# Keeping the third head group's masked scores in PSUM in a fused cross-attention and mixture-of-experts kernel

## The chip, the cores and the metric

One core of a Trainium2 chip runs the whole program. Its engines work side by side, each through its own list of instructions, and wait for each other by semaphores: TensorE (PE; matmuls and transposes, results in PSUM), ScalarE (ACT), VectorE (DVE), GpSimd (POOL), and the queue of SyncE (SP), which issues DMAs. SBUF and PSUM are the on-chip memories; PSUM has eight banks of 128 x 512 fp32. The metric is the device time of one execution in microseconds, lower is better.

## The reference

Eight sequences of 112 tokens (hidden size 512) attend to a context of 375 rows of width 128. The causal mask leaves only context rows 0 to 111 in use. Then follows a feed-forward block of eight experts (two per token) and one shared expert. The part that the change touches:

```python
qp = q @ Wq.T
k, v = jnp.split(latent_kv @ Wkv_expand.T, 2, axis=-1)
# 16 heads of 32
scores = jnp.einsum('bhqd,bhkd->bhqk', qh, kh) * inv_sqrt_d
scores = jnp.where(causal, scores, jnp.finfo(scores.dtype).min)
attn = jax.nn.softmax(scores, axis=-1)
out = jnp.einsum('bhqk,bhkd->bhqd', attn, vh)
x = x + out @ Wout.T            # then: x = x + ffn(layernorm(x))
```

## The kernel before

All engines are programmed by hand; the order of the instructions on each is the order of the code. A batch `b` (0 to 7) is one sequence. Its 16 heads are numbered `h = 4c + r`: four *head groups* `r` (0 to 3), each with four heads `c`. Group `r` has the PSUM bank `S[r]`, in which its four heads' scores (112 x 112 each) lie side by side. The other four banks are A, B, CC and D.

One batch goes through these steps:

- `scores(b)` on TensorE (L635): 16 matmuls write all four banks S[0] to S[3]; the last round over `r` tells group by group that it is done.
- `masked(b, r)` on VectorE (L1341): four operations add the mask, negate, and leave each row's extreme in `negmax`. For `r < RP` the result goes back into the bank; for the others into an SBUF tile `score{r}`. `RP` is 2 (L138).
- `exps(b, r)` on ScalarE (L1053): four exponentials, each followed by a read of its accumulator, with the row's sum; input from the bank for `r < RP`, else from `score{r}`.
- `inverse(b, r)` on VectorE (L1347), then `normalised(b, r)`, on GpSimd (L439) except for the first two of batch 0.
- `transposed(b, r)` on TensorE (L624) into bank A or B, `put_pT(b, r)` (L1008 on ScalarE; group 1 from batch 2 on is at L1351 on VectorE) copies it to `probT`.
- `v_proj(b + 1)` and P·V (L773) on TensorE; `put_oT(b)` (L1064) on ScalarE and `oT_lo(b)` (L1379) on VectorE split its result, `out_proj` (L563) uses it.

TensorE's loop over `b` is: `scores(b+1)`, `transposed(b, 0)` and `(b, 1)`, then in batches 0 and 1 projections of queries and keys for the second half, later `out_proj(b-2)`; `transposed(b, 2)` and `(b, 3)`; `v_proj(b+1)`; P·V. ScalarE's is: `put_pT(b, 0)` (and 1 in batches 0 and 1), `exps(b+1, 0)`, in batches 0 and 1 `put_pT(b, 2)` and `(b, 3)`, `exps(b+1, 1)`, later `put_x2T`, `put_pT(b, 2)` and `(b, 3)` here; `exps(b+1, 2)`, `put_oT(b)`, `exps(b+1, 3)`. VectorE's is: `inverse(b+1, 0)`, `put_pT(b, 1)` from batch 2 on, `masked(b+1, 3)`, `inverse(b+1, 1)`, layer-norm and residual work, `put_v(b+1)`, `inverse(b+1, 2)`, `oT_lo(b)`, `masked(b+2, 0)`, `inverse(b+1, 3)`, `masked(b+2, 1)`, `masked(b+2, 2)`.

The waits around the four banks use the same `RP` (L632 and L1337):

```python
pe.wait_ge(s["mask"], R * (b + 1))         # ahead of scores(b + 1): all four groups of b masked
pe.wait_ge(s["exp"], R * (b - 1) + RP)     # in scores(b): exponentials of b - 1, groups below RP
if b > 0 and r >= RP:                      # in masked(b, r): the SBUF tile must have been read
    dve.wait_ge(s["exp"], R * (b - 1) + r + 1)
```

Behind the attention the feed-forward stages run on the same engines; the loads of the experts' weights start when the output projections are done.

Of the kernel before, what the change touches and what calls it, by code (L numbers as in the profile page):

```python
# [43 lines left out]
def build(nc, x, ctxT, wqT, wkvT, woT, gateT, guT, dnT, sguT, sdnT, out):  # L44
# [5 lines left out]
    R = P // HD  # L50
# [84 lines left out]
    kT = [m.inside(att, f"kT{i}", [P, C, W]) for i in range(NBLK)]  # L135
    v_sb = m.inside(att, "v_sb", [SQ, H])
    score_at = [sg_end + 4 * 2 * H, shared_end - 4 * 2 * H]
    RP = 2  # L138
    score = [None] * RP + [m.inside(score_at, f"score{r}", [SQ, C, SQ]) for r in range(RP, R)]
    prob = [m.inside(att, f"prob{r}", [SQ, C, SQ]) for r in range(R)]  # L140
    probT = [m.inside(att, f"probT{r}", [SQ, C, SQ]) for r in range(R)]
# [123 lines left out]
    s = {n: nc.alloc_semaphore(f"s_{n}") for n in names}  # L265
# [3 lines left out]
    with nc.Block() as block:  # L269
# [280 lines left out]
        def _(pe):  # L550
# [55 lines left out]
            def wait_probT(b, r):  # L606
                if b < 2:
                    pe.wait_ge(s["probT"], R * b + r + 1)
                elif r == 1:
                    pe.wait_ge(s["probT_v"], b - 1)  # L610
                else:
                    pe.wait_ge(s["probT"], R * 2 + (R - 1) * (b - 2) + (1 if r == 0 else r))

            def transposed(b, r):
                if b == 0 and r < RP:
                    pe.wait_ge(s["prob"], r + 1)
                else:
                    pe.wait_ge(s["prob_p"], R * b + r + 1 - RP)
                if r == 0:
                    pe.wait_ge(s["Vs"], b + 1)  # L620
                if r >= 2:
                    wait_probT(b, r - 2)
                for c in range(C):
                    ins = pe.transpose((A, B)[r % 2][0:SQ, c * SQ:(c + 1) * SQ], prob[r][:, c, :], ident[0:SQ, 0:SQ])  # L624
                ins.then_inc(s["PT"], 1)

            def scores(b):
# [3 lines left out]
                if b > 0:  # L631
                    pe.wait_ge(s["exp"], R * (b - 1) + RP)  # L632
                for r, c in [(r, c) for c in range(C) for r in range(R)]:
# [82 lines left out]
            for b in range(NB):  # L716
# [9 lines left out]
                if b == 0:  # L726
                    pe.wait_ge(s["KT"], C + 1)
                    k_proj(1, 1, CC)

                transposed(b, 0)  # L730
                if b == 0:
                    pe.wait_ge(s["QT"], C + 2)
                transposed(b, 1)
                if b == 0:
                    q_proj(1, 2, D)
# [9 lines left out]
                if b >= 2:  # L745
# [6 lines left out]
                    early = 9 if b + 1 < NB else 6  # L752
                    out_proj(b - 2, 0, early)
                transposed(b, 2)
                if b >= 3:
                    t2(b - 3, CC)
# [10 lines left out]
                for h in range(NH):  # L767
                    r, c = h % R, h // R
# [237 lines left out]
        def _(act):  # L1006
# [40 lines left out]
            def exps(b, r):  # L1047
# [3 lines left out]
                for c in range(C):  # L1051
                    src = S[r][0:SQ, c * SQ:(c + 1) * SQ] if r < RP else score[r][:, c, :]
                    ins = act.activation(prob[r][:, c, :], src, ACT.Exp, bias=negmax[:, r, c:c + 1], scale=-1.0,  # L1053
# [228 lines left out]
        def _(dve):  # L1282
# [51 lines left out]
            def masked(b, r):  # L1334

                dve.wait_ge(s["S"], R * b + r + 1)
                if b > 0 and r >= RP:  # L1337
                    dve.wait_ge(s["exp"], R * (b - 1) + r + 1)
# [366 lines left out]
```

## Time and profile before

| | us |
|---|---|
| three timed executions | 340.15, 342.38, 342.55 |
| their median | 342.38 |
| the profiled execution, as timed | 341.11 |
| its span, first to last instruction | 339.2 |
| mean granted TensorE clock | 0.995 of full |

Each number below comes from one profiled execution. A stretch is given in microseconds from the start of its span. "Busy" is the time in which an engine worked on at least one instruction; neighbouring instructions overlap by their pipeline, so the price of one more in a row is the distance from start to start, not its duration. Instructions of one line that follow each other may be merged into one row, with their count.

### The profile page before, as it was taken

The page shows a single profiled execution, that of the slowest core. Times are in us where ns is not written, and L with a number is a line of the kernel's source. Part 1 is how long each engine was busy: PE and PEld are TensorE (multiplying, and loading weights), DVE is VectorE, ACT ScalarE, POOL GpSimd, SP SyncE. Part 2 cuts the span into 40 slices and gives each one's busy share as a digit, 9 for nine tenths or more (in the row PEclk, how much of TensorE's full clock was granted, in tenths as well). Part 3 has the DMA queues.
Part 4 walks back from the last instruction along what each step waited for, and adds up shares of the span by engine and source line. Part 5 has one row for each costly group of instructions (what it writes and reads, how often), then busy time and mean ns, then how long its engine had stood idle before and what let it go on. Part 6 is the DMA issues. An engine that isn't in the chain of part 4 may idle for free.

```text
span 339.2 us, 7025 instructions
## 1 busy us (share of the span) xinstructions
PE 323.4 (95%) x2285; PEld 279.1 (82%) x2285; DVE 269.3 (79%) x676; ACT 232.3 (68%) x581; POOL 140.7 (41%) x144
## 2 busy tenths in 40 slices
PE   7999998999999999999999999999999999999981
PEld 6898886777786798989888977888889999899981
DVE  4879779999756268885667999999999999899840
ACT  3666999999844134131225788888898999889831
POOL 3335475888842000343500008767743423432421
PEclk9999999999999999999999999999999999999998
DMA  7999400000004799697599865554555465455243
GB/s 227 376 337 380 142 3 3 3 3 0 3 2 182 266 348 363 272 308 272 220 283 242 247 242 94 122 119 85 99 116 121 85 110 129 97 90 116 46 50 44
DMA packets 31794, 53.00 MB, mean 156 GB/s; under 512 B 7440, under 2 KB 14992, under 8 KB 30736
## 3 DMA queue, kind: packets, MB, share of 16 engines
q1 hardware_dynamic: 27616, 43.34, 39.1%
q0 software_dynamic: 4144, 9.23, 15.7%
q8 instruction: 19, 0.31, 0.4%
q14 instruction: 15, 0.12, 0.1%
HBM read 32.22 MB, written 16.92 MB: 145 GB/s over the span
## 4 chain that ended last, share of the span: by engine, by line
PE 68%; ACT 10%; DMA 8%; DVE 5%; issue 2%; SPq 2%; POOL 2%; POOLq 1%; ACTq 0%; DVEq 0%
PE bank L563 28%; PE bank L893 19%; ACT prob L1053 6%; PE bank L917 4%; DMA out<-y_sb,dest 3%; PE bank L921 3%; DMA w_dn<-dnT 2%; PE bank L624 2%; PE bank L931 2%; PE bank L927 2%; PE bank L787 2%; PE bank L555 2%; SPq L348 1%; PE bank L773 1%; DMA act_w<-act_e 1%
## 5 line engine op out<-in xcount | busy, mean ns | idle before, releaser
L542 POOL DMA_INDIRECT out<-y_sb,dest x21 | 46.5, 2215 | 101.6 <-ACT y_sb L1223 60.3
L1297 DVE TENSOR_TENSOR gu_parts<-w_gu,gu_parts 128x704 fp32r<-128x704 f32 x84 | 77.2, 953 | 0.3 <-ACT gu_parts L1008 0.3
L1008 ACT ACTIVATE gu_parts<-w_gu 128x704 fp32r x84 | 66.0, 792 | 10.9 <-PE bank L893 10.2
L893 PE MATMUL bank<-gu_parts,xsT_hi 128*128 128x352 f32 x328 | 71.0, 338 | 0.0
L893 PEld LDWEIGHTS bank<-gu_parts,xsT_hi 128*128 128x128 f32 x328 | 54.3, 188 | 5.5 <-issue 4.1
L893 PE MATMUL bank<-gu_parts,xsT_lo 128*128 128x352 f32 x164 | 39.6, 322 | 0.0
L563 PE MATMUL bank<-x2T_hi,w_sg_lo 128*128 128x512 f32 (+1 forms) x88 | 32.6, 371 | 0.1
L563 PE MATMUL bank<-x2T_hi,w_sg_hi 128*128 128x512 f32 (+1 forms) x88 | 32.0, 363 | 0.0
L563 PE MATMUL bank<-x2T_lo,w_sg_hi 128*128 128x512 f32 (+1 forms) x88 | 31.9, 363 | 0.0
L439 POOL TENSOR_TENSOR prob<-prob,rrow 112x448 f32<-112x448 f32 x30 | 27.4, 933 | 9.9 <-DVE rrow L1347 9.8
L515 POOL DMA_INDIRECT xs_dram<-x2n,slot_i x14 | 14.4, 1026 | 37.1 <-DVE eid L1595 33.2
L893 PEld LDWEIGHTS bank<-gu_parts,xsT_lo 128*128 128x128 f32 x164 | 28.6, 188 | 0.0
L1297 DVE TENSOR_TENSOR dn_lo<-w_dn,dn_hi 128x1024 fp32r<-128x1024 f32 x21 | 25.6, 1218 | 3.3 <-ACT dn_hi L1008 3.3
L1008 ACT ACTIVATE act_s_hi<-act_s 128x512 fp32r<-128x512 f32 (+1 forms) x10 | 5.8, 577 | 31.7 <-DVE act_s L1494 24.7
L1514 DVE TENSOR_TENSOR xres<-xres,bank 128x512 f32<-128x512 f32 x35 | 23.0, 683 | 5.0 <-PE bank L563 4.6
L1008 ACT ACTIVATE dn_hi<-w_dn 128x1024 fp32r x21 | 22.2, 1059 | 5.5 <-PE bank L921 4.2
L1053 ACT ACTIVATE prob<-score,negmax 112x112 f32<-112x112 f32 x64 | 24.5, 419 | 0.0
L1053 ACT ACTIVATE prob<-bank,negmax 112x112 f32<-112x112 f32 x64 | 21.9, 384 | 2.5 <-DVE negmax L1341 2.5
L563 PEld LDWEIGHTS bank<-x2T_hi,w_sg_lo 128*128 128x128 f32 x88 | 16.5, 188 | 4.1 <-issue 1.7
L563 PEld LDWEIGHTS bank<-x2T_hi,w_sg_hi 128*128 128x128 f32 x88 | 16.5, 188 | 1.8
L563 PEld LDWEIGHTS bank<-x2T_lo,w_sg_hi 128*128 128x128 f32 x88 | 16.5, 188 | 1.7
L917 PE MATMUL bank<-dn_lo,actT_split_hi 128*128 128x512 f32 x40 | 16.0, 399 | 1.4 <-DVE dn_lo L1297 0.9
(216 smaller groups left out, 818.8 us busy)
## 6 DMA issues: line engine op xcount, KB each, us to landing
w_gu<-guT SPq DMA_DIRECT2D x8, 1408.0 KB, 9.4
xs_dram<-no_row SPq DMA_DIRECT2D x1, 5460.0 KB, 19.8
xs_in<-xs_dram SPq DMA_DIRECT2D x21, 256.0 KB, 2.9
w_dn<-dnT SPq DMA_DIRECT2D x8, 512.0 KB, 6.4
act_w<-act_e SPq DMA_DIRECT2D x19, 176.0 KB, 2.2
w_sg<-sguT SPq DMA_DIRECT2D x10, 256.0 KB, 5.1
w_dn<-dnT SPq DMA_DIRECT2D x8, 192.0 KB, 7.0
w_sd<-sdnT SPq DMA_DIRECT2D x5, 256.0 KB, 4.8
```

What stands on the lines that cost most here:

```text
L439: pool.tensor_tensor(prob[r][:, :, :], prob[r][:, :, :], rrow[:, r, :].unsqueeze(2).to_broadcast([SQ, C, SQ]), ALU.mult)\
L515: pool.indirect_dma_start(out=xs_dram[:, :], out_offset=bass.IndirectOffsetOnAxis(ap=slot_i[:, k, n:n + 1], axis=0), in_=x2n[:, n, :], in_ ...
L542: pool.indirect_dma_start(out=out[:, :], out_offset=bass.IndirectOffsetOnAxis(ap=dest[:, i, 0:1], axis=0), in_=y_sb[i % 2][:, :], in_offse ...
L555: ins = pe.transpose(dst[:, c * P:(c + 1) * P], src[:, c * P:(c + 1) * P], ident[:, :])
L563: ins = pe.matmul(dst, a, b, start=start and n == 0, stop=stop and n == len(passes) - 1)
L893: ins = pe.matmul(dst[:, 0:F], xsT[x_][:, c, :], gu2[w_][:, c, f0:f0 + F], start=c == 0 and n == 0, stop=c == C - 1 and n == 2)
L917: pe.matmul(A[:, :], actT_split[0][:, k, :], dn2[part][:, k, :], start=k == 0 and part == 1, stop=False)
L921: ins = pe.matmul(A[:, :], actT_split[1][:, k, :], dn2[0][:, k, :], start=False, stop=False)
L1008: act.activation(dst, src, ACT.Copy).then_inc(s[sem], 1)
L1053: ins = act.activation(prob[r][:, c, :], src, ACT.Exp, bias=negmax[:, r, c:c + 1], scale=-1.0, accum_out=rowsum[:, r, c:c + 1])
L1297: dve.tensor_tensor(lo_, src, hi_.bitcast(F32), ALU.subtract).then_inc(s[sem], 1)
L1514: dve.tensor_tensor(xres[:, n, :], xres[:, n, :], (B, CC, D, A)[i][:, :], ALU.add)\
```

## The change

`RP` goes from 2 to 3. Group 2's masked scores are written back to bank S[2] in place of an SBUF tile `score2`, the exponentials of group 2 read that bank, `scores(b)` waits for the exponentials of groups 0 to 2 of the batch before, and `masked(b, 2)` has no wait for exponentials any more. In `transposed`, where `RP` stood for the number of groups that VectorE normalises in batch 0, a constant `RN = 2` keeps the value. The order of the instructions is the same on every engine. The SBUF region of `score2` is left free; `score3` and what follows it there lie lower. All lines behind L138 have a number that is one higher.

```diff
-    RP = 2
+    RP = 3
+    RN = 2
     score = [None] * RP + [m.inside(score_at, f"score{r}", [SQ, C, SQ]) for r in range(RP, R)]
...
             def transposed(b, r):
-                if b == 0 and r < RP:
+                if b == 0 and r < RN:
                     pe.wait_ge(s["prob"], r + 1)
                 else:
-                    pe.wait_ge(s["prob_p"], R * b + r + 1 - RP)
+                    pe.wait_ge(s["prob_p"], R * b + r + 1 - RN)
```

## Rows read from the trace of the kernel before

**Rows 1.** Busy time by stretch: us, busy of each engine (instructions), clock, DMA share, GB/s.

```profile
66.00:74.00 8.00, 8.00 (x105) 6.00 (x103) 7.54 (x43) 7.93 (x38) 6.41 (x7) 1.00 0.00 0
90.00:180.00 90.00, 89.88 (x502) 75.43 (x495) 56.42 (x118) 30.89 (x58) 23.32 (x36) 1.00 0.69 244
...
331.00:334.00 3.00, 0.97 (x10) 0.83 (x8) 0.00 (x0) 0.95 (x2) 1.27 (x1) 1.00 0.09 16
334.00:339.00 5.00, 0.00 (x0) 0.00 (x0) 0.00 (x0) 0.00 (x0) 0.28 (x1) 0.69 0.43 52
```

**Rows 2.** Chain of waits, batch 2: start us, us, what.

```profile
47.47 1.75 ACT prob L1053 x9
...
50.45 0.44 ACT oT_hi L1064
...
54.26 0.60 DVE probT L1351
```

**Rows 3.** TensorE's timeline: L635 is `scores`, L624 `transposed`; idle time before in brackets.

```profile
33.11 1.05 PE L635 MATMUL bank<-kT,qT 32*112 32x112 f32 x32 [0.15 <-ACT prob L1053]
...
38.30 0.93 PE L624 MATMUL bank<-ident,prob 112*112 112x112 f32 x8
...
41.34 1.05 PE L635 MATMUL bank<-kT,qT 32*112 32x112 f32 x32
...
45.86 0.93 PE L624 MATMUL bank<-ident,prob 112*112 112x112 f32 x8
...
49.13 1.05 PE L635 MATMUL bank<-kT,qT 32*112 32x112 f32 x32
...
55.00 0.57 PE L624 MATMUL bank<-ident,prob 112*112 112x112 f32 x4 [0.63 <-DVE probT L1351]
...
57.80 1.05 PE L635 MATMUL bank<-kT,qT 32*112 32x112 f32 x32
```

**Rows 4.** Chain of waits, end of batch 5.

```profile
79.62 0.60 ACT probT L1008
80.26 0.96 PE bank L563 x3
```

**Rows 5.** ScalarE's timeline, batch 0: start us, us, engine, line, operation, out<-in.

```profile
32.48 0.40 ACT L1053 ACTIVATE prob<-bank,negmax 112x112 f32<-112x112 f32 x1
32.71 0.25 ACT L1053 ACTIVATION_READ_ACCUMULATOR prob<-bank,negmax 112x1 f32 x1
32.81 0.43 ACT L1053 ACTIVATE prob<-score,negmax 112x112 f32<-112x112 f32 x1
```

**Rows 6.** Steady batches, both timelines: ahead of `transposed(5, 2)`, and of `scores(7)`.

```profile
77.66 0.40 PE L563 MATMUL bank<-w_o_hi,oT_hi 128*128 128x512 f32 x1
78.03 0.60 PE L624 MATMUL bank<-ident,prob 112*112 112x112 f32 x4
...
81.21 0.44 ACT L1053 ACTIVATE prob<-score,negmax 112x112 f32<-112x112 f32 x1
...
81.58 0.43 ACT L1053 ACTIVATE prob<-score,negmax 112x112 f32<-112x112 f32 x1
81.86 0.25 ACT L1053 ACTIVATION_READ_ACCUMULATOR prob<-score,negmax 112x1 f32 x1
82.06 1.05 PE L635 MATMUL bank<-kT,qT 32*112 32x112 f32 x32
```

**Rows 7.** VectorE's timeline, masked scores of batch 3 (groups 0, 1, 2, 2).

```profile
51.46 0.27 DVE L1341 CUSTOM_DVE_ANT_0 bank<-bank,mask 112x112 f32<-112x112 f32 x1
...
53.12 0.32 DVE L1341 CUSTOM_DVE_ANT_0 bank<-bank,mask 112x112 f32<-112x112 f32 x1
...
53.35 0.27 DVE L1341 CUSTOM_DVE_ANT_0 score<-bank,mask 112x112 f32<-112x112 f32 x1
...
53.55 0.27 DVE L1341 CUSTOM_DVE_ANT_0 score<-bank,mask 112x112 f32<-112x112 f32 x1
```

**Rows 8.** ScalarE's timeline: `put_pT` of groups 2 and 3, batches 0 and 1.

```profile
38.88 0.98 ACT L1008 ACTIVATE probT<-bank 112x448 f32<-112x448 f32 x2
...
46.62 1.03 ACT L1008 ACTIVATE probT<-bank 112x448 f32<-112x448 f32 x2
```

## Prediction

> **What bounds the kernel now.** I read four views, in this order. First, the busy time by stretch, to see which stages have room. From 90 us on TensorE is busy for 89.88 of 90 us, with the clock granted in full [rows 1]: whatever moves the end of the attention stage moves the whole program behind it, one for one. From about 28 to 90 us the stage of the change runs, one batch in about 8 us, and there TensorE (8.00 of 8 us), ScalarE (7.93) and VectorE (7.54) are all nearly full [rows 1]. No single engine bounds it. What counts is the loop of waits between them.
>
> Second, the chain of waits says which loop. Up to 50.9 us it runs through ScalarE, whose exponentials and copies follow each other without a gap, then over `oT_lo` and the masked scores on VectorE to `probT` at 54.26 [rows 2], for which TensorE waits 0.63 us [rows 3]. From batch 3 on it alternates: ScalarE from `put_oT(b-1)` to `put_pT(b, 2)`, then TensorE's `v_proj` (80.26) and P·V [rows 4], which release the next `put_oT`. The exponentials of group 2 stand behind `put_pT(b, 3)`, in the shadow of `v_proj` and P·V, so they are not in that loop.
>
> Third and fourth, the timelines of ScalarE and VectorE for the price of one operation, and TensorE's for the place of each `scores`.
>
> **The change part by part.** No instruction moves on any engine. Three things change.
>
> (1) *ScalarE reads group 2 from PSUM.* From start to start, an exponential out of PSUM takes 0.33 us (32.48 to 32.81) [rows 5], one out of SBUF 0.37 us (81.21 to 81.58) [rows 6]. Four of them save 0.16 us a batch.
>
> (2) *VectorE writes group 2's masked scores to PSUM.* Start to start 0.23 us (53.12 to 53.35) against 0.20 us (53.35 to 53.55) [rows 7], so it pays 0.03 to 0.04 each, 0.15 us a batch. Its wait on the exponentials of the batch before goes, but that costs nothing now: nobody waited there.
>
> (3) *`scores(b+1)` waits for the exponentials of groups 0 to 2 of batch b, no longer 0 and 1.* S[2] holds the masked scores until ScalarE has read them, and `scores` overwrites all four banks. Everything behind it on TensorE (`transposed`, the projections, `v_proj`, P·V) waits with it, for TensorE takes its matmuls in order. The Trainium skill, "PSUM — Partial Sum Buffer", section "Summary: rules for kernel authors", says the same of the hardware: a bank that is being read must not be the target of a matmul at that time, and the guard goes by bank. So no looser wait is possible with this placement. By that page alone the wait is necessary, and only the rows tell whether it is also late.
>
> How late it is, batch by batch. The last exponential's accumulator read ends 0.48 us after the exponential starts (32.48 to 32.71 + 0.25 = 32.96), and TensorE starts 0.15 us later, at 33.11 [rows 3, 5].
>
> *scores(1).* Today it already waits for group 1 (that 0.15 us of idle time has ScalarE as its releaser) [rows 3]. Now it waits for group 2, which starts at 32.81: four at 0.33, the last at 33.80, ended at 34.28, `scores(1)` at 34.43. That is 1.32 us later. From there to `transposed(0, 2)` at 38.30 TensorE has no gap to give back, and ScalarE's copy of that result at 38.88 comes 0.58 us behind it [rows 3, 8]. So the copy moves to 40.20. ScalarE has nothing else it may do: the copies stand ahead of `exps(1, 1)` in its order. The head start from (1) is eaten by that wait.
>
> *scores(2).* From 40.20: two copies 0.85 (46.62 to 47.47 in a later batch) [rows 2, 8], group 1 4 x 0.33 = 1.32, group 2's last exponential 0.99 later, at 43.36, ended 43.84, `scores(2)` at 43.99 where it was at 41.34: 2.65 late. `transposed(1, 2)` moves from 45.86 to 48.51 [rows 3], ScalarE's copy to 49.09 (46.62 before) [rows 8]: 2.47 late, since 0.18 us of room was there.
>
> *scores(3).* From 49.09: 0.85 + 1.32 + 0.99 = 52.25, ended 52.73, `scores(3)` at 52.88 where it was at 49.13 [rows 3]: 3.75 late. Not all of it counts, because VectorE was the late one here. `masked(3, 0)` began at 51.46 [rows 7], and now waits for `scores(3)`: its matmuls run 1.05 us [rows 3] and the hand-over takes about 0.10, so it begins at 54.03, 2.57 late. From there VectorE needed 2.80 us to start `put_pT(2, 1)` at 54.26 [rows 2, 7]; with (2) it needs 2.95. That copy starts at 56.98, and `transposed(2, 3)` 0.74 us behind it, at 57.72 where it was at 55.00 [rows 3]: 2.72 late.
>
> *scores(4) and on.* `scores(4)` comes 2.80 us behind it, at 60.52 (57.80 before) [rows 3]. ScalarE, by the same terms, is through with group 2 of batch 3 by 57.72 + 0.58 + 0.42 + 0.99 + 0.48 + 0.15 = 60.34. So the new wait is hidden from here, by 0.18 us. In the steady batches it is nearer. At `scores(7)` the exponentials ended at 81.86 + 0.25 = 82.11; (1) makes that about 81.96 and with 0.15 the release 82.11, against a start at 82.06 [rows 6]. About 0.05 to 0.1 us late each time. Behind it stands a wait that absorbs this: `transposed(b, 2)` started at 78.03 where the matmul ahead of it started at 77.66 [rows 6], 0.37 us for what takes 0.23, thus 0.14 us of waiting on GpSimd. Should that cover be gone, four batches at 0.1 us make 0.4. (2) likewise lies in VectorE's own waits there; (1) saves time only in ScalarE's wait ahead of `put_oT`.
>
> Sum: +1.32 + (2.65 - 1.32 - 0.18) + (2.72 - 2.47) = about **+2.7 us**, all of it between 33 and 58 us. Beside the profiled execution's own 341.11 us this is 343.8. The timed runs lie at 340.15, 342.38 and 342.55; with the profiled one the middle is 341.75, so I say 344.4.
>
> **The rivals.**
>
> *The new wait is on the steady path too* (0.13). The rows leave only 0.05 to 0.18 us between cover and cost at four batches. If the hand-over takes 0.2 to 0.3 us more than at 33.11, each pays that: +0.8 to +1.2, 345.2 to 345.6, and with the late copies of (2) up to 346.8. For it: the margins above. Against: `transposed(b, 2)` waits for GpSimd, not for `scores`.
>
> *TensorE's clock falls* (0.03). TensorE would idle ahead of three `scores`: 0.15 + 1.32, 2.65 - 1.32 and 3.75 - 2.47, so about 1.5, 1.3 and 1.3 us. The trace keeps the full grant with 0.97 us of work in 3 us, and shows 0.69 only in the 5 us behind it without any matmul [rows 1]. A fall from 2.4 to 1.2 GHz over a 4 us stretch that is full would cost up to 4 us: 348. The Trainium skill, "TensorE: Matmul & The Clock Gate", section "What's actually happening", has idleness bring the throttle back; by that rule a stage with more gaps is exposed, but the trace's gap of 2 us at full grant speaks against it here.
>
> *The waits are mostly absorbed* (0.16). ScalarE may have more room at the copies of batches 0 and 1 than I see. Then only `scores(1)`'s 1.32 or less arrives, less the saving of (1) in three batches, 0.48: 341.75 + 1.32 - 0.48 = 342.6.
>
> *The saving of (1) decides, faster than before* (0.03). If ScalarE's order alone set the stage, as the chain suggests up to 50 us, 32 exponentials at 0.04 us give 1.3 us: 341.75 - 1.28 = 340.5. It decides if `scores` is never late by over its cover, 0.15 us; the first one is at 1.32 [rows 3, 5]. The Trainium skill's table of op costs ("VectorE: DVE Perf Modes", section on the TRN2 errata) gives ScalarE 224 cycles of fixed cost from SBUF and 172 from PSUM. The trace agrees in size. By that table alone the estimate is 32 x 52 cycles at 1.2 GHz, 1.4 us faster.
>
> **How the numbers follow.** The forecast (0.65) has its own range, 343.6 to 345.2: the three steps by 0.1 us each, and the half us that executions differ. The range 342.3 to 346.8 takes in most of the absorbed case and the steady one; it leaves out the clock and the faster case. One per cent, about what a measurement of this kernel can tell from no change, is 3.4 us. The forecast reaches it only at its upper edge or through the spread of the runs (0.06 of its 0.65); the steady and clock cases add 0.16. So slower 0.22, within 0.76, faster 0.02.
>
> **What would show it.** Right: idle time of over 1 us on TensorE ahead of the second, third and fourth `scores`, released by ScalarE's `prob`; ScalarE no longer full between 35 and 50 us, with waits for TensorE's transposes at the copies; `scores(4)` near 60.5 us; from there a period of 8.0 to 8.1 us as now. Exponentials from PSUM at 0.33 us in group 2, masked scores at 0.23. Wrong: `scores(4)` before 59 us (absorbed), a period over 8.2 us (steady path), or a granted clock below 1.00 between 33 and 60 us.

## The result, and the profile after

The changed kernel takes 343.35 us (median of 17 executions, 341.78 to 344.43), the kernel before 340.31 us (17 executions, 339.08 to 342.55). The ratio is 1.0082, 95% interval 1.0068 to 1.0096: 2.8 us slower (2.3 to 3.3; the medians lie 3.0 apart). The profiled execution spans 341.4 us at a mean granted clock of 0.996.

Three views of the changed kernel carry the reading. First the busy time by stretch (us, then PE, PEld, DVE, ACT, POOL, granted clock, DMA share, GB/s):

```profile
28.00:40.00 12.00, 10.43 (x114) 9.82 (x115) 11.00 (x70) 8.97 (x45) 6.77 (x9) 1.00 0.77 273
40.00:50.00 10.00, 8.39 (x108) 7.08 (x106) 6.43 (x41) 8.35 (x39) 5.91 (x6) 1.00 0.01 2
50.00:58.00 8.00, 6.36 (x89) 4.88 (x88) 6.36 (x42) 8.00 (x43) 4.30 (x6) 1.00 0.01 2
...
66.00:74.00 8.00, 7.98 (x102) 6.04 (x99) 7.59 (x44) 7.81 (x38) 6.41 (x8) 1.00 0.01 2
...
90.00:180.00 90.00, 89.89 (x523) 74.56 (x522) 57.34 (x128) 32.52 (x69) 24.79 (x39) 1.00 0.66 235
```

From 66 to 74 us TensorE's and VectorE's busy times are those of before to within 0.05 us, and ScalarE is a little less busy (7.81 us where [rows 1] has 7.93). From 90 to 180 us TensorE is as full as before; VectorE and ScalarE differ there by 0.9 and 1.6 us, since the attention stage now ends at 93.30 us, further into this stretch than the 90.09 of before. The holes are before 58 us: ScalarE works for 8.35 of the 10 us from 40 to 50. In the kernel before it had worked for all ten:

```profile
40.00:50.00 10.00, 9.49 (x164) 7.86 (x162) 7.09 (x43) 10.00 (x52) 6.89 (x7) 1.00 0.01 2
```

Second, TensorE's timeline, each `scores` (now L636) and the `transposed` of groups 2 and 3 (L625), with the idle time before it and who ended it:

```profile
28.04 1.05 PE L636 MATMUL bank<-kT,qT 32*112 32x112 f32 x32 [0.28 <-ACT qT L1025]
...
34.99 1.05 PE L636 MATMUL bank<-kT,qT 32*112 32x112 f32 x32 [1.53 <-ACT prob L1054]
...
44.60 1.05 PE L636 MATMUL bank<-kT,qT 32*112 32x112 f32 x32 [1.36 <-ACT prob L1054]
...
53.52 1.05 PE L636 MATMUL bank<-kT,qT 32*112 32x112 f32 x32 [1.36 <-ACT prob L1054]
...
58.18 0.57 PE L625 MATMUL bank<-ident,prob 112*112 112x112 f32 x4 [0.21 <-DVE probT L1352]
...
60.98 1.05 PE L636 MATMUL bank<-kT,qT 32*112 32x112 f32 x32
```

These answer to [rows 3]. The idle times of 1.53, 1.36 and 1.36 us, where before had 0.15 us and none, are all three ended by ScalarE's exponentials. In this execution everything started late, before the stage of the change: `scores(0)` stands at 28.04, in the one of before at 27.51. So I measure from `scores(0)`.

Third, ScalarE's timeline at the copies of transposed groups (L1009): groups 0 and 1 of batch 0, then groups 2 and 3 of batches 0 and 1, which answer to [rows 8]:

```profile
37.28 0.98 ACT L1009 ACTIVATE probT<-bank 112x448 f32<-112x448 f32 x2 [0.58 <-PE bank L625]
...
40.79 0.98 ACT L1009 ACTIVATE probT<-bank 112x448 f32<-112x448 f32 x2 [0.51 <-PE bank L625]
...
49.71 0.98 ACT L1009 ACTIVATE probT<-bank 112x448 f32<-112x448 f32 x2 [1.14 <-PE bank L625]
```

ScalarE stood idle here for 0.58, 0.51 and 1.14 us, waiting for transposes that stood on TensorE behind the late `scores`. That is the loop: `scores(b+1)` waits for ScalarE, then ScalarE waits for what stands behind `scores(b+1)`.

The stage, in microseconds from the start of `scores(0)`:

| | before | forecast | after |
|---|---|---|---|
| `scores(1)` | 5.60 | 6.92 | 6.95 |
| `scores(2)` | 13.83 | 16.48 | 16.56 |
| `scores(3)` | 21.62 | 25.37 | 25.48 |
| `transposed(2, 3)` | 27.49 | 30.21 | 30.14 |
| `scores(4)` | 30.29 | 33.01 | 32.94 |
| `scores(7)` | 54.55 | about 57.3 | 57.32 |
| first matmul of the feed-forward | 62.58 | 65.3 | 65.26 |

This stage length, 62.58 us before and 65.26 after (+2.68), is the measure that I use below beside the ratio. The timed ratios have intervals of 0.5 to 1.1 us to either side (1.3 us for the four-group kernel); the stage lengths come from one profiled execution each, so tenths between them may be chance, and they leave out what varies in the loads ahead and in the experts' DMAs behind.

### The profile page after: what moved, and what is told of

The parts are those of the page before. It is cut to its first block, busy times and chain, and to the rows that moved or that the text cites. A ratio compares the mean times of both kernels' runs of the same rounds, so it can differ in the third digit from the quotient of the medians.

```text
span 341.4 us, 7018 instructions
## 1 busy us (share of the span) xinstructions
PE 324.2 (95%) x2285; PEld 280.8 (82%) x2285; DVE 270.4 (79%) x676; ACT 232.0 (68%) x581; POOL 140.5 (41%) x144
## 4 chain that ended last, share of the span: by engine, by line
PE 80%; ACT 6%; DVE 4%; DMA 3%; issue 2%; POOL 2%; POOLq 1%; ACTq 0%; SPq 0%; DVEq 0%
PE bank L564 33%; PE bank L894 22%; PE bank L918 5%; PE bank L625 3%; ACT prob L1054 3%; PE bank L922 3%; PE bank L636 2%; PE bank L928 2%; PE bank L932 2%; PE bank L788 2%; PE bank L556 2%; DMA out<-y_sb,dest 1%; DMA w_kv<-wkvT 1%; PE bank L774 1%; PE bank L968 1%
## 5 line engine op out<-in xcount | busy, mean ns | idle before, releaser
L1009 ACT ACTIVATE gu_parts<-w_gu 128x704 fp32r x84 | 66.0, 792 | 11.1 <-PE bank L894 10.2
L1054 ACT ACTIVATE prob<-bank,negmax 112x112 f32<-112x112 f32 x96 | 32.8, 378 | 2.5 <-DVE negmax L1342 2.5
L1009 ACT ACTIVATE act_s_hi<-act_s 128x512 fp32r<-128x512 f32 (+1 forms) x10 | 5.8, 578 | 31.5 <-DVE act_s L1495 28.8
L1009 ACT ACTIVATE dn_hi<-w_dn 128x1024 fp32r x21 | 22.2, 1059 | 5.0 <-PE bank L922 3.9
L1342 DVE CUSTOM_DVE_ANT_0 bank<-bank,mask 112x112 f32<-112x112 f32 x96 | 22.9, 310 | 1.0 <-PE bank L636 0.8
L1054 ACT ACTIVATION_READ_ACCUMULATOR prob<-bank,negmax 112x1 f32 x96 | 22.2, 231 | 0.0
```

The lines of the kernel that those rows point to most:

```text
L1009: act.activation(dst, src, ACT.Copy).then_inc(s[sem], 1)
L1342: ins = dve.tensor_tensor_reduce(raw if r < RP else score[r][:, c, :], raw, mask[:, :], -1.0, LARGEST, ALU.add, ALU.min, negmax[:, r, c:c ...
```

## The experiments

Two theories stand against each other. The first: the loss is idle time at the wait of `scores(1)` to `scores(3)`, because these stand on TensorE at a time when ScalarE has group 2 still ahead of it. The second: the placement itself costs, through VectorE's dearer writes or something in PSUM that the trace of before does not show. A third question is whether batches 3 to 7 pay.

**The wait alone.** The kernel before, with this edit:

```diff
-                    pe.wait_ge(s["exp"], R * (b - 1) + RP)
+                    pe.wait_ge(s["exp"], R * (b - 1) + RP + 1)
```

> The kernel before with one edit: scores(b) waits for the exponentials of three groups, the masked scores of group 2 stay in SBUF. Theory (the wait is the loss): scores(1) to scores(3) are late as in the changed kernel and a little more, since group 2's exponentials keep their 0.37 us: 0.16 us later at each of the three waits; VectorE keeps its cheaper masked scores. The three waits then give about +2.7 + 3 x 0.16 - 0.15 = +3.0 us against before, and idle times of about 1.6 us ahead of scores(1) to (3). Rival (the loss comes from VectorE's dearer writes to PSUM, 0.15 us a batch on its path): under +1 us.

Measured: ratio 1.0111 (1.0079 to 1.0143), +3.8 us (2.7 to 4.9); stage +2.82 us. TensorE's timeline:

```profile
34.53 1.05 PE L635 MATMUL bank<-kT,qT 32*112 32x112 f32 x32 [1.64 <-ACT prob L1053]
...
44.24 1.05 PE L635 MATMUL bank<-kT,qT 32*112 32x112 f32 x32 [1.48 <-ACT prob L1053]
...
53.27 1.05 PE L635 MATMUL bank<-kT,qT 32*112 32x112 f32 x32 [1.48 <-ACT prob L1053]
```

The whole loss is there, with nothing moved into PSUM and every buffer in SBUF where it was before. Each idle time is 0.11 or 0.12 us longer than in the changed kernel: that is what ScalarE's faster reads gave back at this place (three intervals of 0.04 us, since only the intervals up to the last exponential count). By one execution each, the placement itself thus gains 0.14 us in the stage.

**By batches.** `in_psum(b)` replaces `RP` in the exponentials, in the masked scores and in the wait of `scores`:

```diff
+    in_psum = lambda b: 3 if b < 3 else 2      # or b >= 3, or b < 1
...
-                    pe.wait_ge(s["exp"], R * (b - 1) + RP)
+                    pe.wait_ge(s["exp"], R * (b - 1) + in_psum(b - 1))
...
-                    src = S[r][0:SQ, c * SQ:(c + 1) * SQ] if r < RP else score[r][:, c, :]
+                    src = S[r][0:SQ, c * SQ:(c + 1) * SQ] if r < in_psum(b) else score[r][:, c, :]
```

Batches 0 to 2:

> The change in batches 0 to 2 alone (placement and wait), batches 3 to 7 as before. Theory (all of the loss arises at scores(1) to scores(3), the steady batches cover the wait): +2.6 to +2.8 us against before, the same as the whole change, and the steady period stays about 8.05 us. Rival (steady batches pay 0.2 to 0.3 us each): about +1.6 us, the rest of the whole change's 2.8 missing.

Measured: 1.0084 (1.0053 to 1.0115), +2.9 us; stage +2.53 us (65.11). Nearly all of the loss.

Batches 3 to 7:

> The change in batches 3 to 7 alone. Theory: -0.2 to +0.2 us against before, scores(4) to (7) wait hardly, ScalarE's saving lands in its idle time ahead of put_oT. Rival (steady batches pay): +0.8 to +1.2 us.

Measured: 1.0031 (1.0008 to 1.0053), +1.1 us (0.3 to 1.8); stage +0.17 us (62.75). The two disagree. In the trace the stage is as long as expected, and `scores(4)` to `scores(7)` have periods of 8.24, 8.03 and 8.10 us (58.86 to 67.10, 75.13, 83.23), where before had 8.14, 8.02 and 8.10. What the timed runs have on top of it, if it is not their spread, isn't in this stage. The sum of both parts by time, 3.9 us, is more than the whole change's 2.8, which the intervals allow. I leave it at that: the trace shows 0.17 us, but the timed interval lies wholly above zero and reaches from 0.3 to 1.8 us, so where the rest of that time lies stays open.

Batch 0 alone:

> The change in batch 0 alone: only scores(1) waits for three groups. Theory (each of the three waits adds its own delay, and what is lost once is not given back): from the first scores to the end of the last P·V the stage takes 1.3 to 1.4 us longer than before (62.6 us there), and the whole +1.3 us; scores(2) and scores(3) have no idle time of their own. Rival (a single early delay is absorbed by room further on, and only three in a row show): under +0.5 us.

Measured: 1.0020 (1.0001 to 1.0038), +0.7 us (0.0 to 1.3); stage +1.37 us (63.95). The stage moved as expected: `scores(1)` idle for 1.50 us, and no idle time at `scores(2)` and `scores(3)`. One early delay of 1.3 us goes through to the end of the stage. By time it is lower, with the forecast 1.3 at the edge of the interval.

**Taking away the wait, first try.** In the changed kernel, `scores(1)` to `scores(3)` in two parts, of which the first waits for the exponentials of groups 0 and 1 alone:

```diff
-                    pe.wait_ge(s["exp"], R * (b - 1) + RP)
-                for r, c in [(r, c) for c in range(C) for r in range(R)]:
+                    pe.wait_ge(s["exp"], R * (b - 1) + min(RP, groups[-1] + 1))
+                for r, c in [(r, c) for c in range(C) for r in groups]:
...
-                    scores(b + 1)
+                    scores(b + 1, range(2) if b < 3 else range(R))
...
                 transposed(b, 1)
+                if b < 3:
+                    scores(b + 1, range(2, R))
```

> The changed kernel, but scores(1) to scores(3) are issued in two parts: groups 0 and 1 where they stood, waiting for the exponentials of groups 0 and 1 alone, and groups 2 and 3 behind transposed(b, 1), by when group 2's exponentials are done. What makes TensorE wait is taken away, the placement in PSUM stays in all batches. Theory: the three idle times of 1.4 us vanish; left are ScalarE's saving of up to 0.5 us in three batches, VectorE's 0.15 us, and the price of matmuls that share the array with one other row group in place of three, 0 to 0.9 us of TensorE in each of three batches, of which TensorE's position ahead of the copies of batch 0 and 1 passes some on: -0.3 to +1.2 us against before, at any rate 1.5 us under the changed kernel. Rival (the placement itself costs, not the wait): +2 us or more.

Measured: 1.0057 (1.0039 to 1.0075), +1.9 us; stage +2.08 us. Worse than the range, and by the stage where the rival said it would be, so this run alone decides nothing. Of the three idle times 0.19 us is left at the first, but:

```profile
33.35 1.04 PE L636 MATMUL bank<-kT,qT 32*112 32x112 f32 x16 [0.19 <-ACT prob L1056]
...
35.90 1.04 PE L636 MATMUL bank<-kT,qT 32*112 32x112 f32 x16
```

Each half takes 1.04 us, as long as the undivided 1.05 (the trace has two records for each of the 8 or 16 matmuls). The control, the same split on the kernel before (`RP = 2`):

> The kernel before (groups 0 and 1 in PSUM, 2 and 3 in SBUF), with scores(1) to scores(3) issued in two halves as in split_early. It prices the split by itself. If the split is what is left in split_early (a half of 16 matmuls on two row groups took 1.04 us, as long as the whole of 32 on four, so 1.04 us more on TensorE in three batches), the stage takes 2.0 to 2.4 us longer than before, the same as split_early or up to 0.3 us more. If the placement in PSUM is what is left there: about +0.5 us or less here.

Measured: 1.0052 (1.0032 to 1.0073), +1.8 us; stage +2.09 us (64.67). The same to 0.01 us. So what is left in the split version is the split's price, and with the wait out of the way the third group in PSUM costs nothing, and gains nothing.

**Second try.** `scores(1)` to `scores(3)` undivided, but behind `transposed(b, 1)`:

```diff
-                    pe.wait_ge(s["mask"], R * (b + 1))
-                    scores(b + 1)
+                    if b >= 3:
+                        pe.wait_ge(s["mask"], R * (b + 1))
+                        scores(b + 1)
...
                 transposed(b, 1)
+                if b < 3:
+                    pe.wait_ge(s["mask"], R * (b + 1))
+                    scores(b + 1)
```

> The changed kernel, with scores(1) to scores(3) undivided but moved behind transposed(b, 1), so that work stands ahead of the wait in place of idle time. Theory (the idle time at the wait is the loss): TensorE idles under 0.5 us ahead of each of the three, the stage takes 0.3 to 1.3 us longer than before (what is left is that VectorE gets the scores of the next batch 0.4 to 1.6 us later, and the 0.15 us of its dearer writes), so 1.4 us or more under the changed kernel's +2.7. Rival (the placement in PSUM costs by itself): +2 us or more.

Measured: 1.0089 (1.0063 to 1.0115), +3.0 us; stage +2.71 us (65.29). A miss. Its control with two groups in PSUM:

> The kernel before (two groups in PSUM) with the same move of scores(1) to scores(3) behind transposed(b, 1). It is the control of transposes_first: once no wait stands in the way, the third group in PSUM should be free or gain ScalarE's 0.16 us in each of three batches less VectorE's 0.15 us. Theory: this control's stage is 0 to 0.5 us longer than that of transposes_first. Rival (PSUM costs by itself): this control is shorter by 0.5 us or more.

Measured: 1.0054 (1.0036 to 1.0072), +1.8 us; stage +2.59 us (65.17), 0.12 us shorter than with three groups, not longer. By time the two are 1.2 us apart, with intervals that overlap. The move is as dear as the wait. TensorE's timeline of the first of the two says why:

```profile
43.19 0.95 PE L625 MATMUL bank<-ident,prob 112*112 112x112 f32 x8 [0.97 <-DVE v_sb L1379]
44.07 1.05 PE L636 MATMUL bank<-kT,qT 32*112 32x112 f32 x32
```

`transposed(b, 0)` writes bank A and must wait until VectorE has copied `v_proj`'s result out of it, which starts when P·V is done. Where `scores` stood between them, it covered that copy. I took the cover away and got 0.97 us of idle time in its place in batches 1 and 2. In batch 0, `scores(1)` starts 8.07 us after `scores(0)` in place of 5.60, and VectorE stands idle for 1.65 us and ScalarE for 0.70 us until its results come. The experiment therefore says nothing on the first theory; it turned one wait into another. By the stages, the pair speaks against the second theory: the third group adds 0.12 us to this order.

**Third try.** Work that waits for nothing is put ahead of the first two waits, and no cover is touched: in batch 0 the key projection and `transposed(0, 0)`, in batch 1 the query projection.

```diff
-                    pe.wait_ge(s["mask"], R * (b + 1))
-                    scores(b + 1)
+                    if b == 1:
+                        pe.wait_ge(s["QT"], C + 3)
+                        q_proj(1, 3, D)
+                    if b > 0:
                         pe.wait_ge(s["mask"], R * (b + 1))
                         scores(b + 1)
...
                 transposed(b, 0)
+                if b == 0:
+                    pe.wait_ge(s["mask"], R * (b + 1))
+                    scores(b + 1)
...
                 if b == 1:
-                    pe.wait_ge(s["QT"], C + 3)
-                    q_proj(1, 3, D)
```

> The changed kernel (three groups in PSUM), with independent work put ahead of the first two waits: the key projection and transposed(0, 0) ahead of scores(1), the query projection of batch 1 ahead of scores(2); scores(3) as in the changed kernel. Theory (idle time at the wait is the loss): idle ahead of scores(1) falls from 1.5 to about 0.3 us, ahead of scores(2) to nothing; scores(3) still waits, since it goes by ScalarE's place; VectorE's chain behind scores(3) then is about 1.0 us late. Stage from the first scores to the feed-forward's first matmul: +0.7 to +1.4 us against before, where the changed kernel has +2.7. Rival (whatever stands ahead, ScalarE's order sets the stage): +2 us or more.

Measured: 1.0036 (1.0013 to 1.0060), +1.2 us; stage +1.15 us (63.73). Of the loss of 2.68 us, 1.53 are gone. The idle times of the first two waits have vanished, the third is what it was, as expected:

```profile
35.32 1.05 PE L636 MATMUL bank<-kT,qT 32*112 32x112 f32 x32
...
44.69 1.05 PE L636 MATMUL bank<-kT,qT 32*112 32x112 f32 x32
...
52.34 1.05 PE L636 MATMUL bank<-kT,qT 32*112 32x112 f32 x32 [1.36 <-ACT prob L1059]
```

The control, the same two moves on the kernel before:

> The kernel before (two groups in PSUM) with the same two moves: what the moves cost by themselves. Theory: scores(2) starts about 2.1 us later for the query projection ahead of it, which ScalarE's room of 0.2 us ahead of its next exponentials doesn't cover whole: +0.3 to +0.9 us in the stage, so that 0.2 to 0.8 us of the loss in filled is the third group's, mostly at scores(3). Rival (the moves are free): 0 +/- 0.2 us, and all that is left in filled is the third group's.

Measured: 1.0019 (0.9997 to 1.0041), +0.6 us; stage +0.85 us (63.43). The moves cost 0.85 us by themselves, and the third group adds 0.30 us to them, where it added 2.68 without them: nine tenths of its price are gone, though only the first two idle times were taken away. `scores(1)` itself comes no earlier, 6.95 us after `scores(0)` as in the changed kernel; the gain is the work done ahead of it. By time the two versions are 0.6 us apart, inside their intervals. Neither beats the kernel before.

**A wait that no batch can hide.** `RP = 4`, all four groups in PSUM:

> The changed kernel with all four groups in PSUM, so that scores(b+1) waits for exps(b, 3), which stand behind put_oT(b-1) and so behind the P·V of the batch before: the wait can't be hidden in any batch. Theory (what counts is where the last awaited exponential stands in ScalarE's order): scores(1) 2.9 us late, every later scores idle for 0.10 + 0.42 + 0.99 + 0.48 + 0.15 = 2.1 us behind its P·V, of which ScalarE's path passes on 1.7 to 2.1: a period of 9.8 to 10.2 us where it was 8.1, and +13 to +15 us in all. Rival (the wait costs about 1.3 us wherever it stands): +9 us or less.

Measured: 1.0628 (1.0589 to 1.0667), +21.4 us; stage +24.2 us (86.73, in one execution). The direction is as expected, the size isn't, and the timeline of TensorE shows what was missing:

```profile
48.79 1.05 PE L636 MATMUL bank<-kT,qT 32*112 32x112 f32 x32 [3.15 <-ACT prob L1054]
...
61.06 1.85 PE L636 MATMUL bank<-kT,qT 32*112 32x112 f32 x32 [3.14 <-ACT prob L1054]
62.84 1.74 PE L625 MATMUL bank<-ident,prob 112*112 112x112 f32 x8
...
65.26 0.63 PE L564 MATMUL bank<-w_o_hi,oT_hi 128*128 128x512 f32 x1
65.69 0.63 PE L564 MATMUL bank<-w_o_hi,oT_lo 128*128 128x512 f32 x1
...
67.31 0.39 PE L564 MATMUL bank<-w_o_lo,oT_hi 128*128 128x512 f32 x1
67.54 0.40 PE L564 MATMUL bank<-w_o_hi,oT_hi 128*128 128x512 f32 x1
...
84.69 1.05 PE L636 MATMUL bank<-kT,qT 32*112 32x112 f32 x32 [2.10 <-ACT prob L1054]
...
94.69 1.85 PE L636 MATMUL bank<-kT,qT 32*112 32x112 f32 x32 [2.16 <-ACT prob L1054]
```

And its busy time by stretch:

```profile
60.00:70.00 10.00, 8.94 (x63) 7.47 (x63) 5.61 (x39) 5.80 (x30) 3.17 (x4) 0.66 0.00 1
70.00:80.00 10.00, 7.84 (x95) 6.79 (x95) 6.95 (x43) 6.22 (x33) 6.53 (x7) 0.83 0.01 2
80.00:90.00 10.00, 7.88 (x100) 6.20 (x100) 7.72 (x41) 8.05 (x38) 5.61 (x6) 1.00 0.01 2
```

The idle time of 2.1 us in the steady batches came as forecast. Two things did not. First, ahead of `scores(2)` and `scores(3)` the idle time was 3.15 and 3.14 us, about 1 us more at each than the 2.1 that I expected everywhere. Second, the granted clock fell. Behind an idle time of 3.14 us a 512-column matmul starts 0.43 us after the one ahead of it, later 0.23 us: the lower level, 1.2 GHz, then 2.4 GHz again. The batch at full clock (84.69 to 94.69, 10.0 us) has the expected period of 9.8 to 10.2, 2.0 us over before; the ones from 61.06, 73.17 and 94.69 us, each with a fall, are 3.3 to 3.4 us over theirs. So a fall cost about 1.4 us there. As an estimate, `scores(1)` 3.1 us late, idle times of 3.15 and 3.14 us and four batches at +2.0 make 17 us of the 24, and the falls the other 7. In this kernel idle time had a second price. The Trainium skill, "TensorE: Matmul & The Clock Gate", section "What's actually happening", has idleness bring the throttle back. By that rule, the trace agrees: 0.66 granted between 60 and 70 us.

## Why the prediction was right

By its own steps:

- *The base.* I took 341.75 for the kernel before from four executions; seventeen say 340.31, which is 1.44 us less. The forecast difference was 2.65 us (344.4 less 341.75), the measured one 2.8 (2.3 to 3.3). The measured 343.35 lies inside the wide range of 342.3 to 346.8, but just below the 343.6 to 345.2 that I gave the forecast itself, and the base is why. As an absolute time it lies nearly as close to the absorbed case at 342.6. What tells them apart is the difference, 2.3 to 3.3 us where that case has 0.84, and the stage.
- *(1) and (2), the prices of one operation.* VectorE's masked scores of group 2 show 0.23 us from start to start (56.42 to 56.65 in batch 3), ScalarE's exponentials 0.33 (33.35 to 33.68). As forecast.
- *(3), "no looser wait is possible".* This holds only for undivided `scores`. The split version waits more loosely and was no gain, since the division cost 2.09 us of its own.
- *scores(1) to (3).* 1.35, 2.73 and 3.86 us late against 1.32, 2.65 and 3.75. The small rest is in part hundredths that each step hands on: from the start of the last exponential to `scores` it takes 0.64 or 0.65 us (34.34 to 34.99, 43.96 to 44.60, 52.88 to 53.52) where I had 0.63. The copies of ScalarE behind them are 1.38 and 2.56 us late against 1.32 and 2.47.
- *VectorE as the late one in batch 2.* `transposed(2, 3)` 2.65 us late, forecast 2.72. That it came so near is partly luck, for three small terms were off. `scores(3)` was 0.11 us later than forecast, but the hand-over to VectorE took nothing (53.52 + 1.05 = 54.57, the start of `masked(3, 0)`) in place of 0.10. From there VectorE needed 2.87 us to its copy (57.44) in place of 2.95: in the kernel before it had waited 0.07 us in between, and this took up half of (2). Only 0.21 us of idle time is left ahead of the transpose, since TensorE itself was late.
- *The cover from `scores(4)` on.* Forecast: `scores` 0.05 to 0.1 us late in the steady batches, absorbed by the wait for GpSimd. Measured: `scores(5)` to `scores(7)` 2.76 or 2.77 us late, P·V between them 2.67 or 2.68, the end of the stage 2.68. The tenth is there each time and is given back each time. The period from `scores(4)` to `scores(5)` is 8.25 us (60.98 to 69.23), over the 8.2 that I had named as a sign of the steady path. It was a poor sign, for the kernel before has 8.14 there; the next two are 8.02 and 8.11.
- *The savings of (1) there.* They went into ScalarE's idle time ahead of `put_oT`: 0.19 us ahead of the one at 85.41, against 0.08 us at the same place before (82.11 to 82.19). The wait alone, without the placement, has a stage 0.14 us longer.
- *The rivals.* Steady batches that pay: not in any trace (+0.17 us in batches 3 to 7), though the timed runs of that experiment leave room for it. The clock: 1.00 in all stretches of the changed kernel's attention stage, with idle times up to 1.53 us. It may have been nearer than I gave it: in the four-group kernel it fell behind two idle times of 2.16 us. Absorbed: batch 0's delay alone arrived whole in the stage. Faster by ScalarE's saving: `scores` was late by far more than its cover.

Three of my expectations were wrong in ways that belong to the same reasoning. In the first try I gave a split at most 0.9 us a batch, and each extra half took 1.04 us. In the second try I moved work ahead of a wait and did not ask what the moved instruction had been covering. In the four-group kernel I priced idle time as time alone, and took the steady batches' 2.1 us for the early ones too.

## What to carry to other kernels

When a result stays in the buffer that its producer overwrites next, find where the last reader stands in its engine's order, and compare that moment with the moment at which the producer comes round again, batch by batch: here the wait cost 1.4 and 1.2 us at the first two places and another 0.1 at the third, and nothing in the steady batches, where the producer had other work first. Here, a faster access on the reading engine (0.04 us of 0.37) was worth only what it moved on the path that released the next step. Before moving work ahead of a wait, look up which copy or transfer it hides where it stands.

## What the runs showed of the hardware

- Scores with 32 rows in use: 16 matmuls over four row groups take 1.05 us, and 8 over two row groups 1.04 us. Splitting them by group gave no time back; that the row groups work side by side is my reading of this.
- The granted clock of TensorE stayed at 1.00 with idle times of 1.36 to 1.64 us before `scores` (the changed kernel and the wait alone). In the four-group kernel it stood at the lower level for part of the next batch behind each idle time of 3.1 to 3.2 us and behind two of four of 2.1 to 2.2 us (those of 2.16, not those of 2.10). Four cases don't show whether these 0.06 us decide. Such a fall added about 1.4 us to a batch: 11.44 us from 94.69 to 106.13, where before has 8.10, against 10.00 from 84.69 to 94.69, where before has 8.02.
